# Queries of the second attention projected from the rows between the layers, with shift and deviation applied afterwards

## What is computed

```
x = x + tanh(g_xattn[0]) * attention0(layernorm(x), ctx)
x = x + tanh(g_ffn[0])   * selections(layernorm(x))      # one row for each sequence, added to all its rows
x = x + tanh(g_xattn[1]) * attention1(layernorm(x), ctx, mask)   # with rotary positions
x = x + tanh(g_ffn[1])   * experts(layernorm(x))         # 16 experts and a shared one
```

## Time and profile before

| | |
|---|---|
| median of three runs | 793.22 us |
| profiled execution: its time | 789.21 us |
| profiled execution: its span, first to last instruction | 787.4 us |
| busy: TensorE, its weight loads | 682.1 us (87%), 548.8 us (70%) |
| busy: VectorE, ScalarE, GpSimd | 452.6 us (57%), 334.4 us (42%), 218.9 us (28%) |
| mean granted TensorE clock | 0.956 |

### The profile page before, as it was taken

The page is one execution under the profiler, slowest core; times in us unless marked ns, Lnnn a source line. Parts: engine busy times, 40 slices in busy tenths (PEclk is TensorE's granted clock), DMA queues, the critical chain, the costliest instruction groups (busy, mean ns, idle before and its releaser), DMA issues.

```text
span 787.4 us, 13684 instructions
## 1 busy us (share of the span) xinstructions
PE 682.1 (87%) x5104; PEld 548.8 (70%) x5104; DVE 452.6 (57%) x919; ACT 334.4 (42%) x757; POOL 218.9 (28%) x200
## 2 busy tenths in 40 slices
PE   5889988999987637775999998999988899999998
PEld 4667655778864334443666665899976799999997
DVE  4758755110127465667467545545877777788713
ACT  3455655556641201113344555322227566555510
POOL 6635311000000500057254321000105545544500
PEclk9999999999998856998799999999999999999999
DMA  7865660670000223014334440400000455566313
GB/s 269 237 175 163 173 181 2 254 304 16 0 0 1 92 112 105 1 40 124 94 103 127 113 129 2 161 1 1 1 1 1 160 189 197 194 225 225 113 34 107
DMA packets 61479, 87.22 MB, mean 111 GB/s; under 512 B 17265, under 2 KB 50801, under 8 KB 60401
## 3 DMA queue, kind: packets, MB, share of 16 engines
q1 hardware_dynamic: 60624, 85.90, 34.1%
q10 hardware_dynamic: 800, 0.59, 0.2%
HBM read 63.54 MB, written 18.73 MB: 104 GB/s over the span
## 4 chain that ended last, share of the span: by engine, by line
PE 74%; DVE 11%; issue 6%; ACT 4%; POOL 3%; DMA 2%; ACTq 0%; DVEq 0%; POOLq 0%
PE ps L924 72%; DVE keep L1741 2%; DMA keep<-in_x 1%; ACT big L674 1%; DVE keep L1752 1%; PE ps L930 1%; POOL kbr L505 1%; ACT keep L684 1%; DVE keep L1734 1%; DVE keep L1749 1%; POOL vp L546 1%; PE ps L1400 1%; DVE mcol L1558 0%; DMA m_rows<-big 0%; ACT vp L674 0%
## 5 line engine op out<-in xcount | busy, mean ns | idle before, releaser
L924 PE MATMUL ps<-keep 128*128 128x120 bf16 (+9 forms) x517 | 83.9, 286 | 39.8 <-DVE keep L1741 30.8
L924 PEld LDWEIGHTS ps<-keep 128*128 128x128 bf16 (+2 forms) x517 | 42.2, 119 | 68.1 <-DVE keep L1741 43.8
L924 PE MATMUL ps<-thi,whi 128*128 128x256 f32 x256 | 73.8, 288 | 3.9 <-POOL tlo L603 2.1
L924 PE MATMUL ps<-thi,wlo 128*128 128x256 f32 x256 | 72.4, 283 | 0.0
L924 PE MATMUL ps<-tlo,whi 128*128 128x256 f32 x256 | 72.4, 283 | 0.0
L768 ACT ACTIVATE ps<-ps 128x256 f32<-128x256 f32 x128 | 47.6, 372 | 38.6 <-PE ps L924 38.6
L924 PE MATMUL ps<-qpair,kpair 98*77 98x256 f32 x256 | 57.9, 341 | 3.8 <-ACT big L674 2.2
L505 POOL TENSOR_TENSOR kbr<-khi,keep 128x616 fp32r<-128x616 f32 x32 | 40.9, 1300 | 65.9 <-PE ps L924 63.6
L837 ACT ACTIVATE att<-ps 128x512 f32<-128x512 f32 x48 | 28.6, 596 | 68.6 <-PE ps L924 68.3
L924 PE MATMUL ps<-xhi,phi 128*128 128x512 f32 x128 | 50.7, 396 | 2.9 <-ACT ps L768 2.9
L924 PEld LDWEIGHTS ps<-thi,whi 128*128 128x128 f32 x256 | 48.9, 191 | 5.8 <-issue 3.4
(11 more groups left out here) (219 smaller groups left out, 1812.0 us busy)
## 6 DMA issues: line engine op xcount, KB each, us to landing
qpair<-q_rows SPq DMA_DIRECT2D x16, 768.0 KB, 5.7
q_rows<-qhi SPq DMA_DIRECT2D x32, 256.0 KB, 2.7
big<-in_piw SPq DMA_DIRECT2D x4, 2048.0 KB, 12.4
q_rows<-qlo SPq DMA_DIRECT2D x16, 256.0 KB, 2.7
att<-in_wg SPq DMA_DIRECT2D x8, 512.0 KB, 3.6
att<-in_wu SPq DMA_DIRECT2D x8, 512.0 KB, 4.4
att<-in_wd SPq DMA_DIRECT2D x8, 512.0 KB, 5.2
big<-in_wg SPq DMA_DIRECT2D x8, 512.0 KB, 3.6
```

The lines of the kernel that those rows point to most:

```text
L924: return pe.matmul(out, lhsT, rhs, start=start, stop=stop, skip_group_check=True)
```

## The change

The query projection is linear, so it can be made from rows that aren't normalised yet, and not even complete. Let y be the rows between the layers, after the first attention and before the selections' row r is added. With weights whose mean over the input is taken out (Wc), `layernorm(y + r) @ Wq.T = ((y + r) @ Wc.T) / deviation = (y @ Wc.T + r @ Wc.T) / deviation`.

- In the first search TensorE turns y of all sequences (`turn_mid`, 4 transposes each) and sums the weights (`sum_weights`); ScalarE copies the turned rows (`copy_mid`). After it GpSimd takes the mean out of the weights, ahead of rotating the keys.
- In the second and third search, and ahead of each, TensorE projects the queries (`project_mid`, 16 halves of a sequence), and ScalarE copies them (`copy_projected`) to `qmid`.
- After the selections the row r is projected for all sequences at once (8 columns); ScalarE copies the result (`shift`).
- For each sequence of the second attention GpSimd writes 1/deviation on the diagonals of two matrices (`spread`); TensorE multiplies them by ones, which gives 1/deviation along the row in all partitions (`scale_rows`); VectorE adds the shift and multiplies (`scale_queries`), into `qpre`; ScalarE adds the bias from there. Normalisation, transposes, copy and projection of these sequences are gone.
- The order changes: the swap takes the projection's place behind key_scores 0-1, `scale_rows(n+3)` the swap's; bias and `rotary_a` are done one sequence earlier; `block_keys` is first in GpSimd's order; `stats` of sequence n+4 comes behind the rotation and the low part of n+2 on VectorE. In the order written out ahead of the loop, `stats(10)` comes behind `low_rotated(8)`, `rotary_b(9)` stays ahead of the second maxima of 8.

```diff
+            def spread(n):
+                pool.wait_ge(rstd_done, n + 1)
+                if n >= B + 2:
+                    pool.wait_ge(q_ps, n - 1)
+                pool.tensor_tensor(diag[n % 2], ident.unsqueeze(1).to_broadcast([P, 2, P]),
+                                   rstd[:, n % 2].unsqueeze(2).to_broadcast([P, 2, P]), ALU.mult).then_inc(diag_done, 1)
@@ attend on GpSimd
+                    if layer == 1 and n + 3 < hi:
+                        block_keys(n + 3)
                     if n + 4 < hi:
                         inv_std(n + 4)
-                    if layer == 1 and n + 2 < hi:
-                        rotary_a(n + 2)
-                    if n + 3 < hi:
+                        if layer == 1:
+                            spread(n + 4)
+                    if layer == 1 and n + 3 < hi:
+                        rotary_a(n + 3)
@@ GpSimd after the first search
             pool.wait_ge(tk_cnt, 28)
+            pool.wait_ge(mid_act, 1)
+            pool.tensor_tensor(wq, wq, wmean.unsqueeze(1).to_broadcast([P, DC, D]), ALU.add).then_inc(wq_done, 1)
@@ GpSimd ahead of the loop
             block_keys(8)
             inv_std(8)
+            spread(8)
             inv_std(9)
+            spread(9)
+            rotary_a(8)
             inv_std(10)
-            rotary_a(8)
+            spread(10)
+            block_keys(9)
             rotary_a(9)
-            block_keys(9)
             add_value_bias(0, 4)
             block_keys(10)
+            rotary_a(10)
             inv_std(11)
+            spread(11)
@@ TensorE
+            def scale_rows(m):
+                pe.wait_ge(diag_done, m - B + 1)
...
+                mm(ps[:, scale_bank(m), 0:S], onesf, diag[m % 2].rearrange("p t q -> p (t q)")).then_inc(q_ps, 1)
+            def turn_mid(b):
...
+                transpose_tokens(5 + b % 2, x_sb[:, tiles(b), :]).then_inc(midT_ps, 1)
+            def project_mid(i):
+                b, g = divmod(i, 2)
...
+                for c in range(DC):
+                    ins = mm(ps[:, mid_bank(b), S * g:S * g + S], wq[:, c, P * g:P * g + P], midT[:, b, c, :],
+                             c == 0, c == DC - 1)
-            top_k(0, 16, [(keys, j) for j in range(4)] + [(swapped_keys, j) for j in range(4)])
+            top_k(0, 16, [(keys_and_mid, j) for j in range(4)] + [(swaps_and_mid, j) for j in range(4)])
-            top_k(1, 8, [(all_maxima, 0), (all_maxima, 1)])
+            for i in range(2):
+                project_mid(i)
+            top_k(1, 8, [(maxima_and_queries, i) for i in range(8)])
-            top_k(2, 16, [(half_values, i) for i in range(8)])
+            for i in range(10, 12):
+                project_mid(i)
+            top_k(2, 16, [(values_and_queries, i) for i in range(8)])
@@ attend on TensorE
                     if m < hi:
-                        project_q(m)
+                        if layer == 0:
+                            project_q(m)
+                        else:
+                            swap_pairs(m)
...
-                        else:
-                            swap_pairs(m)
+                    elif n + 3 < hi:
+                        scale_rows(n + 3)
...
-                    if n + 3 < hi:
+                    if n + 3 < hi and layer == 0:
                         pe.wait_ge(max_done, 2 * n + 6)
                         transpose_xn(n + 3)
@@ VectorE
+            def scale_queries(m):
...
+                for g in range(2):
+                    at = B * g + m - B
+                    ins = dve.scalar_tensor_tensor(out=qpre[:, g], in0=qmid[:, m - B, g, :], scalar=shift[:, at:at + 1],
+                                                   in1=ps[:, scale_bank(m), 0:S], op0=ALU.add, op1=ALU.mult)
@@ attend_second on VectorE
-                    if n + 4 < 2 * B:
-                        stats(n + 4)
-                        normalise(n + 4)
...
                         rotary_b(n + 2)
+                    if n + 3 < 2 * B:
+                        scale_queries(n + 3)
+                    if n + 2 < 2 * B:
                         low_rotated(n + 2)
+                    if n + 4 < 2 * B:
+                        stats(n + 4)
@@ ScalarE after the first search
             gelu_columns(2)
+            copy_projected(0)
             high_keys(3)
+            copy_projected(1)
```

More of the change, by code:

```diff
@@ L93, in flamingo_kernel @@
         xnT_b = xnT_b_s.rearrange("p (c t) -> p c t", c=DC)
+        diag = [xn_s[:, 2 * P * j:2 * P * j + 2 * P].rearrange("p (t q) -> p t q", t=2) for j in range(2)]
+        rowT, shift, wmean = xn_s[:, 512:528], xn_s[:, 528:544], xn_s[:, 768:1024]
+        qpre = xnT_b_s.rearrange("p (g q) -> p g q", g=2)
         cst = keep(C_END)
@@ L707, in attend @@
                         values_out(3, PV_BANK + 1)
+                    if n + 2 < hi and layer == 1:
+                        high_queries(n + 2)
                     exponentials(n, (4, 5))
@@ L810, in _ @@
             gelu_columns(2)
+            copy_projected(0)
             high_keys(3)
+            copy_projected(1)
             act.wait_ge(sm_dve, 5)
             act.activation(gtm[:, 0:64], gtm[:, 0:64], ACT.Exp).then_inc(sm_act, 1)
+            for b in range(2, 5):
+                copy_projected(b)
             act.wait_ge(oa_ps, 1)
@@ L817, in _ @@
             gelu_columns(4)
-            for j in range(4):
-                values_out(4 + j, j % 2)
+            copy_projected(5)
+            values_out(4, 0)
+            copy_projected(6)
+            values_out(5, 1)
+            values_out(6, 0)
+            copy_projected(7)
+            values_out(7, 1)
             act.preload_act_table_set("natural_log_exp_and_others")
@@ L829, in _ @@
             maxima_out(8)
-            copy_xt(10)
+            raw_queries(10)
             attend(1)
@@ L1030, in weigh_values @@
                     pe.wait_ge(mT_done, n + 2)
+                if c == 1 and layer == 1 and b + 3 < B:
+                    pe.wait_ge(q_pre, b + 4)
                 pe.wait_ge(v_done, 4 * layer + b // 2 + 1)
@@ L1180, in half_values, with sum_weights, keys_and_mid, swaps_and_mid @@
                     ins.then_inc(v_ps, 1)
+            def turn_mid(b):
+                if b == 0:
+                    pe.wait_ge(x_done, B)
+                elif b >= 2:
+                    pe.wait_ge(midT_done, b - 1)
+                transpose_tokens(5 + b % 2, x_sb[:, tiles(b), :]).then_inc(midT_ps, 1)
+            def sum_weights():
+                for c in range(DC):
+                    ins = mm(ps[:, 0, 0:D], onesf, wq[:, c, :], c == 0, c == DC - 1)
+                ins.then_inc(mid_pe, 1)
+            def project_mid(i):
+                b, g = divmod(i, 2)
+                if b == 0:
+                    pe.wait_ge(wq_done, 1)
+                    pe.wait_ge(midT_done, B)
+                elif b in (2, 3, 4, 7):
+                    pe.wait_ge(qmid_done, b - 1)
+                for c in range(DC):
+                    ins = mm(ps[:, mid_bank(b), S * g:S * g + S], wq[:, c, P * g:P * g + P], midT[:, b, c, :],
+                             c == 0, c == DC - 1)
+                if g == 1:
+                    ins.then_inc(qmid_ps, 1)
+            def keys_and_mid(j):
+                keys(j)
+                turn_mid(j)
+            def swaps_and_mid(j):
+                swapped_keys(j)
+                turn_mid(4 + j)
+                if j == 3:
+                    sum_weights()
+            def maxima_and_queries(i):
+                if i < 2:
+                    all_maxima(i)
+                project_mid(2 + i)
+            def values_and_queries(i):
+                if i == 0:
+                    pe.wait_ge(qmid_done, 5)
+                half_values(i)
+                if i % 2 == 0:
+                    project_mid(12 + i // 2)
             def all_maxima(step):
@@ L1534, in low_queries @@
                 ins.then_inc(qlo_done, 1)
+            def scale_queries(m):
+                dve.wait_ge(q_ps, m + 1)
+                if m == B:
+                    dve.wait_ge(mid_act, 3)
+                    dve.wait_ge(qmid_done, B)
+                else:
+                    dve.wait_ge(q_raw, m - B)
+                for g in range(2):
+                    at = B * g + m - B
+                    ins = dve.scalar_tensor_tensor(out=qpre[:, g], in0=qmid[:, m - B, g, :], scalar=shift[:, at:at + 1],
+                                                   in1=ps[:, scale_bank(m), 0:S], op0=ALU.add, op1=ALU.mult)
+                ins.then_inc(q_pre, 1)
             def rotary_b(m):
```

103 lines of the change are left out of this document (72 added, 31 removed).

## The result

| | before | after |
|---|---|---|
| median of the timed runs | 792.22 us (788.96 to 794.64, 4 runs) | 773.92 us (772.98 to 774.41, 4 runs) |
| profiled execution, its span | 789.21 us, 787.4 us | 774.41 us, 772.6 us |
| its mean granted clock | 0.956 | 0.971 |

The account below looks back on a forecast made before the run. TensorE was taken to bound the second attention's regular part, VectorE's search the selections. Terms −10.3 (regular part), −10.3 (start), +1.7 (selections) gave −18.9 us, from 793.2 to 774 us; range 765 to 786.

Parts of the forecast that it names:

- Regular part, 14.4 us a step (10.3 in all): Second attention, maxima of 10 to 15: TensorE's queue loses 1.74 + 0.41 + 0.35 − 0.44 = 2.06 us per sequence, five steps.
- An instruction taken off its queue there shortens the kernel: Second attention's regular part: TensorE is busy 78.09 of 82.10 us at clock 1.00, so removing its instructions shortens the kernel.
- VectorE's margin of 0.4 us: Regular part: VectorE needs 5.0 us after the swap, TensorE some 5.4, so the maxima were expected on time.
- Rival A: Regular part: another wait takes over, each sequence loses 1.3 of its 2.06 us, total 781 us; chance 0.14.
- Scaling 0.84 us for two: VectorE, each sequence of the second attention: two scalings of 256 columns take 0.84 us, replacing normalisations of 1.69 us.
- Start, 10.3 us: Start of the second attention: 11.3 us gained up to maxima of 10, 1 us taken off for clock lost to new stops.
- its own signs of being wrong: Among them: a maxima wait over 1 us ahead of row scores or their turning; idle TensorE over 3 us behind maxima of 9.
- the stop ahead of the row scores of 10: Start of second attention: TensorE's 5.16 us stop, rotation standing behind normalising 12; new order removes it, plus 3.98 us of clock.
- GpSimd's lateness: Start of second attention: GpSimd, waiting for statistics of 10, leaves VectorE dry some 3 us ahead of rotation sum of 9.
- Selections, +1.7: Three selections: added transposes, centring and projections cost 1.7 us together, between −4 and +11.
- half of 3.6: Second selection: projections keep the clock up, 2.8 us in steps and about 0.8 in aggregation; half taken, −1.8 (−4 to +3).
- The end, 0: Behind the maxima of 15, unchanged work: no change in time forecast.

Follow-up runs that it names:

- e8: Kernel before, query projection and transposes of sequences 11 to 15 each cut to one product of 8 columns: 794.39 us (ratio 1.0038).
- e7: Changed kernel, query scaling of sequences 11 to 15 done twice on VectorE, the first time into an unread buffer: 780.61 us (ratio 0.9817).
- e4: Kernel before with only the new order at the start of the second attention, on VectorE and GpSimd: 792.35 us (ratio 1.0003).
- e9: e8's kernel with the normalisation of sequences 12 to 15 also cut to 8 of 256 columns on VectorE: 793.54 us (ratio 1.0027).
- e5: Changed kernel, statistics of sequence 10 moved ahead of the rotation of 8 on VectorE: 768.15 us (ratio 0.9705).
- e3: Changed kernel without the sixteen half-batch projections, 8 products of 8 columns in their place: 776.94 us (ratio 0.9833).
- e10: Kernel before with twenty unused products of 256 columns on TensorE, ahead of and in the second selection: 788.88 us (ratio 0.9982).
- e12: e5's kernel with two output-row additions moved earlier, plus two half projections moved ahead and unused products in TensorE's gaps: 767.50 us (ratio 0.9704).
- e6: Changed kernel, query weights centred on GpSimd behind the third rotated key block instead of ahead of the first: 772.40 us (ratio 0.975).
- e2: Changed kernel run again unchanged, for a second trace: 773.36 us (ratio 0.9789).
- e1: Kernel before run again unchanged, for a second trace: 791.19 us (ratio 1.0014).

## Why the prediction was right, point by point

- **Regular part, 14.4 us a step (10.3 in all): measured 14.1 and 11.6.** Right by the TensorE queue: projection, transposes and the wait of 0.35 us gone, new product 0.46 for 0.44. The remaining 0.3 us a step lie in places where the sum had kept the old spacing: from the swap's start to the next scores 0.86 instead of 0.97, from the output projection to the row scores 1.54 instead of 1.72, and 0.91 instead of 1.09 for the score group behind the projection.
- **"An instruction taken off its queue there shortens the kernel": wrong as a rule.** e8 took nearly 2 us of products off and the step grew by 0.6. The bound held because normalising left VectorE in the same change: in e8 the steps without a normalisation are the ones that got shorter. The prediction saw such a stop at the start of the attention, and missed that the loop was one product away from it.
- **VectorE's margin of 0.4 us: right as idle time, wrong as margin.** 0.42 us of idle time was there; the margin was 0.16, because the statistics release a chain on GpSimd, and VectorE's copy ahead of the second maxima is held until that chain ends (e7). The prediction had called GpSimd's queue hidden. Rival A was nearer than its reasons said.
- **Scaling 0.84 us for two: 0.87.** The low part behind it took 0.69 where it had been 0.77.
- **Start, 10.3 us: measured 8.4** (the -9.0 and the +0.6). The stop went, and the row scores of 10 and later ran at the full clock (1.00 from 366 us on). But the new stops ahead of the maxima of 8 (3.66 us) left the row scores of 9 at the low clock: about 0.5 in 356 to 366 us. The prediction took 1 us for that. A wait of over 1 us ahead of the turning of maxima is also one of its own signs of being wrong; it came at this one place (1.67 us before), not in the loop. Its reason for the stop ahead of the row scores of 10, the order, was not enough: the order alone gave 0.7 us (e4), a short normalisation in the old order 4.9 (e9 against e8). GpSimd's lateness was there, 1.75 us instead of 3, and e5 took it away.
- **Selections, +1.7: measured -3.3.** The step that failed: what the added products cost in time and give back in clock. In the first selection the transposes, forecast at 1.2 us, cost nothing (from its first count to the first process product 28.0 and 27.9 us before, 28.0 and 27.7 after). The clock was higher with them, and the process products behind took 7.11 us instead of 8.69; but TensorE then stood 2.95 us for ScalarE's copy instead of 0.51, since the copy hung on GpSimd's centring and key blocks. So of the forecast +2.2 (1.2 for the transposes, 1.0 for the centring) +1.0 came, the centring's. The second selection gained 3.1 us where half of 3.6 had been taken: the clock went up with the first count and was 0.88 over the stretch in both traces, although the second has a low spell behind a gap of 1.74 us. The third gained 1.1 where 1.3 were to be lost: the products between the values kept the clock at 1.00 through it (0.88 before).
- **The end, 0: measured +3.7.** Behind the maxima of 15 the program is the same. Over the eight runs that have the new loop this part takes 322.3 to 326.6 us, mean 324.8; over the four with the old loop 320.5 to 322.4, mean 321.7. A stop with no releaser in the combination of routed tokens lasts 4.20 us in seven of the eight and 2.94 in the eighth, and 2.94, 3.00, 0.49 and 3.02 us in the four; e8 and e9, whose loop is cut, have 4.2 too. The rest are waits of 1 to 2 us for expert weights, at changing places. Why the stop has several sizes stays open, and so does whether the change has to do with it; that 3 us of the unchanged end are chance alone is not shown.

So the loop's gain was understood and came a little larger, but that the total fell on 774 us is luck: the selections' 5.0 us in excess and the loop's 1.3 made up for the start's 1.9 and the 6.1 of the unchanged parts. With the selections as forecast the time would have been 779 us, with unchanged ends 768: both inside the range of 765 to 786 us, neither at its middle.

## What to carry to other kernels

Taking work from the busiest engine pays in full only if the engine that feeds it has room at the same place: cut the work crudely first (e8) and look which wait appears. Idle time in front of a wait is not a margin if something behind the late instruction runs through another engine. Real work put into the gaps of a stretch that another engine paces can cost less than nothing, since it keeps TensorE's clock (e3, e10); but work moved forward leaves its gap behind (e12).

## What the runs showed of the hardware

- Some VectorE operations from SBUF to SBUF that begin while GpSimd works are held until GpSimd's instruction ends, almost whatever their size: 2.40 us for two normalising operations of 8 columns (e9; 0.48 with GpSimd idle), 2.57 for two of 256 (e8), 0.56 and 1.17 for a copy of 4 columns (after, e7; 0.17 with GpSimd idle, at 57.58 us), 0.70 instead of 0.20 for 64 integers (e6).
- The statistics, which read SBUF as well, are not. Beside GpSimd's multiplications from 399.62 to 402.14 us this one took 0.41 us, as it did at 56.85:

```profile
400.88 0.41 DVE L1628 BATCH_NORM_STATS2 keep<-keep 128x6 f32<-128x256 f32 x1
```

- The operations seen here with an operand in PSUM are not held either. In e5 two scalings took 0.87 us while GpSimd was busy throughout, and the SBUF subtraction behind them 1.34 instead of 0.69:

```profile
343.21 0.87 DVE L1683 SCALAR_TENSOR_TENSOR keep<-big,keep,ps 128x256 f32<-128x256 f32 x2
344.14 1.34 DVE L1701 TENSOR_TENSOR qlo<-big,qhi 128x512 fp32r<-128x512 f32 x1
```

```profile
343.04 0.72 POOL L545 TENSOR_TENSOR keep<-keep 128x256 f32<-128x256 f32 x1
343.73 2.83 POOL L519 TENSOR_TENSOR kbr<-khi,keep 128x616 fp32r<-128x616 f32 x2
```

- With counts of 1.08 us and gaps of mostly 1.2 to 1.7 us TensorE stays at 1.2 GHz for 32 us (clock 0.50, e3); with half projections in them and gaps of 0.70 us most of the stretch runs at 2.4 GHz (0.88 as a mean, after and e10).
- Transposes seem to keep the clock as well. In the first selection the only new work on TensorE is 32 of them and, at its end (260.04 us), four instructions of 256 columns for the weights' sum. From 3 us behind the first count to the process products the clock is 0.98 and 0.99 (after, e2), without them 0.91 and 0.91 (before, e1). Over all traces: once up, it stays at 1.00 to the end of the process products in the eight with the transposes. Of the six without, four fall to 0.50 behind the fifth step and again at the process products, e4 at the process products only, and e8 not at all. The longer count in the low spell comes after 1.78 us of idle time before, and after 1.36 with the transposes:

```profile
246.52 2.92 PE L924 MATMUL ps<-keep 128*128 128x120 bf16 x19 [1.78 <-DVE keep L1741]
```

```profile
247.25 0.60 PE L988 MATMUL ps<-keep 128*128 128x128 f32 x4
249.21 1.90 PE L982 MATMUL ps<-keep 128*128 128x120 bf16 x19 [1.36 <-DVE keep L1894]
```

The Trainium skill ("TensorE: Matmul & The Clock Gate", section "Part 4: PE-mode transpose") says that the clock's full level doesn't engage for transposes, which don't count as busy in the same way. By it the low spells would have come as often with them as without. The traces speak against it here, none of eight against five of six, for transposes of float32 between matmuls; since one trace without transposes kept its clock too, and transposes alone were not tried, it is not shown beyond that.
